# Mirrored score blocks of a fused attention and MLP block, turned by VectorE and DMA instead of TensorE

## The chip, the core and the metric

The kernel runs on one core of a Trainium2 chip. The core has TensorE (matrix products), VectorE, ScalarE and GpSimd (elementwise work), each with an instruction queue of its own that it works through in order, and SyncE (SP), whose queue here issues every DMA. The metric is the time of one execution in device microseconds (us). Three runs give 693.47, 693.54 and 694.78 us, median 693.54.

## What is computed

Eight batches of 1024 rows and 256 features pass through attention and an MLP, each behind a layer norm with a modulation per batch. All is float32.

```
mod = (_silu(L0_c) @ L0_wmod).reshape(L0_c.shape[0], 6, 1, -1)
sa, ca, ga, sb, cb, gb = (mod[:, 0], ..., mod[:, 5])
h = _layernorm(x) * (1 + ca) + sa
lhs, rhs = h * w_lhs, h * w_rhs
scores = einsum('nsd,ntd->nst', lhs, rhs)
attn = softmax(scores, axis=2)
x = x + ga * einsum('nst,ntd->nsd', attn, h)
h = _layernorm(x) * (1 + cb) + sb
x = x + gb * (relu(h @ W1 + b1) @ W2 + b2)
```

Since lhs and rhs are the same h times a factor per feature, the score matrix is symmetric: block (i, j) of 128 by 128 is block (j, i) turned.

## The kernel before

**Tiling.** A batch is 8 row tiles of 128 rows, so the scores of a batch are 8 × 8 blocks in the tile `S`. The features are two halves of 128 (`DK`), the hidden layer 8 tiles of 128, taken over two halves of 512 rows: 16 steps each of the first layer (F) and the second (G). For accuracy every product is made of three matmuls: hi × hi, hi × lo, lo × hi, where hi is a value rounded to fp32r and lo the rest.

**Stages.** Each engine has a list of steps, a kind and a number: `BEFORE_STEPS`, `FIRST_STEPS` (batch 0), `SECOND_STEPS` (batch 1), `STEPS` (batches 2 to 6, a loop), `LAST_STEPS` (batch 7), `AFTER_STEPS`. A suffix "-" means that the step works for the batch before, "+" for the one after: the MLP of a batch runs beside the attention of the next. Every engine goes through its list in order; between engines stand only semaphore waits. Batch 0 goes a way of its own in plain float32.

**The kinds, batches 1 to 7.**
- SC.n, TensorE (L542 to L585): scores of row tile n into one of two PSUM tiles `score`. Rows 0 to 3 make the left half from column `first_col[n]` on (0, 1, 2, 2 blocks in) and all of the right half; rows 4 to 7 only the right half, from 4, 5, 6, 6. What stands left of that start is the mirror of blocks already made and is turned by TensorE with the identity (L584). SC.n waits until VectorE has copied SC.n−2 out (`scores_read`).
- SC.n, VectorE (L864): copies the scores to `S` and takes each row's maximum over them into `row_max`.
- ST.n, VectorE (L896): turns 32 × 32 pieces of the right half of rows 0 to 3 into `stage`. SW and SR, SP (L444, L449): write the stage to DRAM and read it back piece by piece into `lower`, the lower left quarter of the matrix.
- MX, VectorE (L900, L903): the maximum over `lower`, joined to `row_max` of rows 4 to 7.
- MB.0 and MB.1, TensorE (L655): spread the maxima of rows 0 to 3 and 4 to 7 over all partitions, into `max_ps`.
- SB.n, VectorE (L887 to L892): subtracts the maxima from columns n of `S`, in place. EX.n, ScalarE (L793): exponential, in place. SM.n: ScalarE rounds it to `Phi` (L806), VectorE makes the rest `Plo` (L911). AV.n: TensorE multiplies with `V` (L690 to L694), VectorE divides and adds to x (L928) and takes the statistics of the second norm.
- VN, ScalarE (L783): x minus mean into `ln_v`; VL, VectorE (L1038): times rstd and gate, four instructions of one tile each; V: the hi part by ScalarE (L788), the lo part by VectorE (L980).
- L1 and L2: mean and variance on VectorE (L951, L954), −mean and rstd on GpSimd (L1069 to L1072). N1 and N2, GpSimd (L1079): normalise four tiles of 256 columns into `ln_t`. BH and B2, VectorE (L990, L991): turn 32 × 32 pieces of it. SH, RH, S2, R2, SP: carry them through DRAM (`blocks`, `block_rows`). TH and T2: ScalarE and VectorE make the turned features of the attention (`Lhi`, `Rhi`, `Llo`, `Rlo`) and the MLP (`h2hi`, `h2lo`).
- F.n: product on TensorE (L593 to L595), ReLU and hi part on ScalarE (L715, L719), lo part on GpSimd (L1088). G.n: product on TensorE (L530 to L536). OUT, VectorE (L1026, L1030): gate and sum. XG, VectorE (L1051): x plus the gated bias. XC, GpSimd (L1139): x plus the shift of the attention. X0, X1, XT, AM, GA, GB, O0, O1 on SP: loads and stores. WS: ScalarE and GpSimd split the weights, in batch 0; WR: TensorE waits for that. TP: TensorE turns the features of the first MLP half of batch 0.

Of the kernel before, what the change touches and what calls it, by code (L numbers as in the profile page):

```python
# [5 lines left out]
F32 = mybir.dt.float32  # L6
F32R = mybir.dt.float32r
ALU = mybir.AluOpType
# [90 lines left out]
        SC.0 F.0- SC.1 F.1- F.2- SC.2 SC.3 F.3- SC.4 F.4- MB.0 G.0- SC.5 G.1- SC.6 F.5- SC.7 G.2- F.6- G.3-  # L99
        G.4- F.7- G.5- F.8- F.9- G.6- F.10- MB.1 G.7- AV.0 F.11- AV.1 G.8- F.12- G.9- AV.2 G.10- AV.3 F.13-  # L100
        F.14- AV.4 F.15- G.11- AV.5 G.12- AV.6 G.13- G.14- G.15- AV.7
    """,
    "act": """
        F.0- VN.0 F.1- V.0 F.2- T2.1- F.3- VN.1 F.4- EX.0 L1.0+ SM.0 F.5- EX.1 F.6- F.7- EX.2 F.8- V.1 F.9-
        EX.3 SM.1 F.10- TH.0+ SM.2 SM.3 F.11- EX.4 EX.5 SM.4 F.12- SM.5 F.13- TH.1+ F.14- EX.6 MC.0 SM.6
        EX.7 SM.7 F.15- T2.0
    """,
    "dve": """
# [1062 lines left out]
```

## Time and profile before

| | |
|---|---|
| median of three runs | 693.54 us (693.47 to 694.78) |
| profiled execution, its span | 691.5 us (its own time is not given apart) |
| TensorE busy | 686.1 us, 99% |
| VectorE busy | 558.4 us, 81% |
| ScalarE busy | 427.5 us, 62% |
| GpSimd busy | 361.7 us, 52% |
| one middle batch | 82.2 us |
| granted TensorE clock | full in all slices |

The profile is one execution, and its span runs from the first to the last instruction. PE is TensorE's matmuls, DVE VectorE, ACT ScalarE, POOL GpSimd, SP SyncE. Busy time is a union: consecutive instructions overlap a little in the records, since the end of one lies behind the start of the next. So what an instruction in a row costs its engine is the distance to the next start. Idle time of an engine that others don't wait for costs nothing.

### The profile page before, as it was taken

Reading aid. Unit: us, or ns where it says so; the run is one execution under the profiler, and the core shown is the slowest. Engines: PE = TensorE matmul, PEld = TensorE weight load, DVE = VectorE, ACT = ScalarE, POOL = GpSimd, SP = SyncE. Lnnn points to the kernel's source line nnn. Section 1 sums busy time; section 2 is a strip of 40 time slices with the busy share of each in tenths; the row PEclk is TensorE's granted clock in tenths of the full one; section 3 lists DMA queues with packets and bytes.
Section 4 is the critical chain, followed back from the end, with each engine's and each line's share of the span. In section 5 each row is a group of like instructions: output and inputs, shape, how many; then the busy total and the mean of one; then the engine's idle time right before and its main releaser. Section 6 shows DMA issues by size and latency. Waiting matters only on the chain.

```text
span 691.5 us, 13488 instructions
## 1 busy us (share of the span) xinstructions
PE 686.1 (99%) x4621; PEld 627.7 (91%) x4621; DVE 558.4 (81%) x1059; ACT 427.5 (62%) x625; POOL 361.7 (52%) x396
## 2 busy tenths in 40 slices
PE   9999999999999999999999999999999999999998
PEld 8688899998999989998999989999899998999997
DVE  5699989799898898978989799887989887876421
ACT  3265398736786367683786647864678634845562
POOL 3572576636654386352872458643665434523644
PEclk9999999999999999999999999999999999999999
DMA  8211761137431382315622266112843126003300
GB/s 294 81 49 59 204 193 55 39 107 252 123 100 56 103 232 91 99 61 179 180 67 90 67 226 185 61 38 98 258 121 99 46 91 221 1 1 100 100 31 30
DMA packets 61663, 77.54 MB, mean 112 GB/s; under 512 B 5632, under 2 KB 54336, under 8 KB 61632
## 3 DMA queue, kind: packets, MB, share of 16 engines
q1 hardware_dynamic: 61632, 77.14, 35.5%
q8 instruction: 18, 0.29, 0.2%
q14 instruction: 13, 0.11, 0.1%
HBM read 46.15 MB, written 30.97 MB: 112 GB/s over the span
## 4 chain that ended last, share of the span: by engine, by line
PE 94%; DVE 4%; issue 0%; ACT 0%; DMA 0%; DVEq 0%; ACTq 0%; SPq 0%
PE col L595 9%; PE col L594 9%; PE col L593 9%; PE acc L530 8%; PE acc L531 8%; PE acc L536 8%; PE score L694 8%; PE score L690 8%; PE score L691 8%; PE score L578 4%; PE score L579 4%; PE score L580 4%; PE score L576 2%; PE score L584 2%; PE score L499 1%; DVE S L879 1%
## 5 line engine op out<-in xcount | busy, mean ns | idle before, releaser
L1088 POOL TENSOR_TENSOR hid_lo<-hid,hid_hi 128x512 fp32r<-128x512 f32 x127 | 175.4, 1386 | 143.2 <-ACT hid_hi L719 142.8
L715 ACT ACTIVATE hid<-col,b1T 128x512 f32<-128x512 f32 x128 | 87.0, 679 | 140.3 <-PE col L595 126.1
L530 PE MATMUL acc<-W2hi,hid_hi 128*128 128x256 f32 x480 | 119.2, 282 | 0.0
L531 PE MATMUL acc<-W2lo,hid_hi 128*128 128x256 f32 x480 | 116.9, 278 | 0.0
L690 PE MATMUL score<-V,Phi 128*128 128x258 f32 x448 | 108.8, 281 | 0.0
L691 PE MATMUL score<-V,Phi 128*128 128x256 f32 x448 | 108.6, 281 | 0.0
L719 ACT ACTIVATE hid_hi<-hid 128x512 fp32r<-128x512 f32 x128 | 81.0, 633 | 37.6 <-PE acc L536 29.8
L593 PE MATMUL col<-h2hi,W1hi 128*128 128x512 f32 x256 | 102.4, 400 | 0.0
L595 PE MATMUL col<-h2hi,W1lo 128*128 128x512 f32 x256 | 101.0, 395 | 0.0
L594 PE MATMUL col<-h2lo,W1hi 128*128 128x512 f32 x256 | 100.6, 393 | 0.0
L530 PEld LDWEIGHTS acc<-W2hi,hid_hi 128*128 128x128 f32 x480 | 90.4, 188 | 2.1
L531 PEld LDWEIGHTS acc<-W2lo,hid_hi 128*128 128x128 f32 x480 | 90.2, 188 | 1.8
L690 PEld LDWEIGHTS score<-V,Phi 128*128 128x128 f32 x448 | 85.0, 190 | 0.7
L691 PEld LDWEIGHTS score<-V,Phi 128*128 128x128 f32 x448 | 84.0, 188 | 0.6
L1069 POOL TENSOR_SCALAR nm<-mv 128x4 f32<-128x4 f32 x32 | 16.7, 523 | 129.2 <-DVE mv L932 104.2
L911 DVE TENSOR_TENSOR Plo<-S,Phi 128x1024 fp32r<-128x1024 f32 x56 | 70.2, 1269 | 8.1 <-ACT Phi L806 6.4
L536 PE MATMUL acc<-W2hi,hid_lo 128*128 128x256 f32 x480 | 76.6, 276 | 0.0
L864 DVE TENSOR_SCALAR_CACHE_REDUCE S<-score 128x1024 f32<-128x1024 f32 (+1 forms) x64 | 62.7, 980 | 15.2 <-PE score L584 12.9
L793 ACT ACTIVATE S<-S 128x1024 f32<-128x1024 f32 (+1 forms) x64 | 64.4, 1019 | 13.2 <-DVE S L879 7.7
L1139 POOL TENSOR_TENSOR x_cur<-x_cur,attn_mod 128x512 f32<-128x512 f32 x32 | 43.3, 1354 | 40.8 <-DVE ln_v L1038 40.8
L536 PEld LDWEIGHTS acc<-W2hi,hid_lo 128*128 128x128 f32 x480 | 64.6, 188 | 0.0
L694 PE MATMUL score<-V,Plo 128*128 128x258 f32 x448 | 62.8, 282 | 0.0
(139 smaller groups left out, 1493.2 us busy)
## 6 DMA issues: line engine op xcount, KB each, us to landing
block_rows<-blocks SPq DMA_DIRECT2D x29, 512.0 KB, 2.9
blocks<-block_rows SPq DMA_DIRECT2D x116, 128.0 KB, 3.0
x_cur<-x SPq DMA_DIRECT2D x16, 512.0 KB, 3.9
ln_t<-x SPq DMA_DIRECT2D x14, 512.0 KB, 4.8
score_blocks<-stage SPq DMA_DIRECT2D x14, 512.0 KB, 4.2
lower<-score_blocks SPq DMA_DIRECT2D x56, 128.0 KB, 2.9
out<-x_mlp SPq DMA_DIRECT2D x8, 512.0 KB, 3.0
out<-x_mlp SPq DMA_DIRECT2D x15, 256.0 KB, 2.2
```

The source lines that it names most:

```text
L530: nc.tensor.matmul(o, hi, W2hi[:, it, :], start=(it == 0 and (apart or t % 2 == 0)), stop=False, skip_group_check=True)
L531: nc.tensor.matmul(o, hi, W2lo[:, it, :], start=False, stop=False, skip_group_check=True)
L536: last = nc.tensor.matmul(o, lo, W2hi[:, it, :], start=False, stop=(it == FT - 1), skip_group_check=True)
L593: nc.tensor.matmul(col[n % 2][:], W1hi[:, kk, tile], h2hi[:, kk, cols], start=(kk == 0), stop=False)
L594: nc.tensor.matmul(col[n % 2][:], W1hi[:, kk, tile], h2lo[:, kk, cols], start=False, stop=False)
L595: last = nc.tensor.matmul(col[n % 2][:], W1lo[:, kk, tile], h2hi[:, kk, cols], start=False, stop=(kk == DK - 1))
L690: nc.tensor.matmul(o, Phi[:, slot, t, :], V[:, t, 0:VW], start=(t == 0), stop=False)
L691: nc.tensor.matmul(o[:, 0:D], Phi[:, slot, t, :], V[:, t, VP:VP + D], start=False, stop=False)
L694: last = nc.tensor.matmul(o, Plo[:, slot, t, :], V[:, t, VP:VP + VW], start=False, stop=(t == T - 1))
L715: nc.scalar.activation(hid[:, n % 2, :], col[n % 2][:], ACT.Relu, bias=b1T[:, n % FT:n % FT + 1]).then_inc(col_read, 1)
L719: nc.scalar.activation(hid_hi[:, n % RING, :], hid[:, n % 2, :], ACT.Copy).then_inc(hid_hi_done, 1)
L1088: G.tensor_tensor(hid_lo[:, n % RING, :], hid[:, n % 2, :], hid_hi[:, n % RING, :].bitcast(F32), ALU.subtract).then_inc(hid_lo_done, 1)
```

## The change

In batches 1 to 7 TensorE turns no score blocks. It multiplies the right upper quarter whole, and of the two quarters on the diagonal the blocks `QCOLS`: (0, 1, 2), (1, 2, 3), (2, 3), (0, 3) of each row, 10 where it were 11. Six blocks of each quarter are mirrors: VectorE turns their 32 × 32 pieces (QT.0, QT.1, out of `S` into `stage_q`), SP writes them to DRAM (QW) and reads them back piece by piece (QR) into `turned_in`. `S` is packed, so that these blocks fit into it. The maxima have parts (`part_max`): from the copies, from the turned blocks (MX.0 and MX.2) and from the lower left quarter (MX.1); MB.0 and MB.1 both wait for them (`max_ready`). SB reads from `S` and the turned blocks and writes to a ring `soft` of three column tiles, on which EX and SM work. N1 and N2 go from GpSimd to ScalarE, with scale rstd and bias `nb1`, `nb2` = −mean × rstd, a product that GpSimd adds. VN does the whole normalisation, and VL is one instruction for four tiles. All orders are new; batch 0 keeps its steps otherwise.

```diff
 STEPS = {
     "pe": """
-        SC.0 F.0- SC.1 F.1- F.2- SC.2 SC.3 F.3- SC.4 F.4- MB.0 G.0- SC.5 G.1- SC.6 F.5- SC.7 G.2- F.6- G.3-
...
+        SC.0 SC.1 F.0- F.1- SC.2 SC.3 F.2- F.3- SC.4 SC.5 G.0- G.1- F.4- SC.6 G.2- G.3- SC.7 F.5- F.6- MB.0
...
     "sp": """
-        AM.0 GA.0- S2.1- XT.0+ SW.0 R2.1- SR.0 X1.0 SW.1 SR.1 SH.0+ XT.1+ RH.0+ O0.0- SH.1+ RH.1+ GB.0 S2.0
...
+        AM.0 S2.1- XT.0+ R2.1- QW.0 X1.0 SW.0 QR.0 SR.0 SH.0+ SW.1 XT.1+ SR.1 GA.0- RH.0+ QW.1 GB.0 QR.1 SH.1+
...
+    QCOLS = [(0, 1, 2), (1, 2, 3), (2, 3), (0, 3)]
...
+                    elif kind == "QW":
+
+                        sp.wait_ge(quarter_done[n], b)
+                        sp.dma_start(quarter_blocks[n], stage_q[n]).then_inc(quarter_stored[n], 16)
+                    elif kind == "QR":
+
+                        sp.wait_ge(quarter_stored[n], 16 * b)
+                        for u in range(Q):
...
+                        for right in range(0 if n < HT else 1, 2):
...
+                            if not right:
+                                o = score[n % 2][:, 0:HR]
+                            else:
+                                o = score[n % 2][:, HR:HR + len(quarter) * P]
...
+                                elif n % HT == HT - 1:
+                                    whole = slice(n // HT * HR, (n // HT + 1) * HR)
+                                    hi, lo = [r[:, kk, whole].rearrange("p (c q) -> p c q", q=P)[:, ::HT - 1, :] for r in (Rhi, Rlo)]
...
-                        for i in range(left // P, at // P):
-                            if i == at // P - 1:
-                                pe.wait_ge(scores_read, T * b + i + 1)
-                            last = nc.tensor.transpose(score[n % 2][:, i * P:(i + 1) * P], S[:, i, n * P:(n + 1) * P], ident[:])
...
+                            pe.wait_ge(max_ready, 2 * b + n - 1)
...
+                    elif kind == "N1":
+                        act.wait_ge(ln1_rstd, 2 * b + 3 + n)
+                        for t in range(HT):
+                            i = n * HT + t
+                            last = nc.scalar.activation(ln_t[:, t, :], ln_t[:, t, :], ACT.Identity, scale=rs1[:, i:i + 1], bias=nb1[:, i:i + 1])
+                        last.then_inc(ln1_done, 1)
...
+                        V_.tensor_tensor(tile[:, h * HT:(h + 1) * HT][:, rows], kept, most.broadcast_to(list(kept.shape)), ALU.subtract)
...
+                        V_.tensor_tensor(by_quarter(out), turned_q[h][:, turns], by_quarter(most.broadcast_to(list(out.shape))), ALU.subtract)
...
+                    elif kind == "QT":
+
+                        dve.wait_ge(scores_read, T * b + (n + 1) * HT)
...
-                        for t in range(HT):
-                            i = n * HT + t
-                            dve.wait_ge(v_mean, HT * (2 * b + n - 2) + t + 1)
-                            V_.scalar_tensor_tensor(ln_v[:, t, :], ln_v[:, t, :], rs1[:, i:i + 1], attn_mod[:, 0, :], ALU.mult, ALU.mult).then_inc(v_ln, 1)
+                        dve.wait_ge(v_mean, HT * (2 * b + n - 2) + HT)
+                        V_.tensor_tensor(ln_v[:], ln_v[:], attn_mod[:, 0:1, :].broadcast_to([P, HT, D]), ALU.mult).then_inc(v_ln, HT)
```

How the instructions now stand, at three places of the loop body. First TensorE at the end of SC.3; score0 and score1 are the two PSUM tiles, col1 that of the first layer. Before, the end of the products, two transposes, then step F.3:

```order
L580 MATMUL score1<-Rhi,Llo 128x512
L584 MATMUL score1<-ident,S 128x128 x2
L590 REGISTER_ALU
L593 MATMUL col1<-h2hi,W1hi 128x512
L594 MATMUL col1<-h2lo,W1hi 128x512
```

After, the right half of SC.3 is the product of blocks 0 and 3, and step F.2 follows:

```order
L634 MATMUL score1<-Rhi,Lhi 128x256
L635 MATMUL score1<-Rlo,Lhi 128x256
L636 MATMUL score1<-Rhi,Llo 128x256
L642 REGISTER_ALU
L645 MATMUL col0<-h2hi,W1hi 128x512
L646 MATMUL col0<-h2lo,W1hi 128x512
```

The transposes are gone, and the step ends with a product.

Second, TensorE around MB.0, whose instruction writes the maxima to score1. Before, F.4 stands ahead of it and G.0 behind it:

```order
L595 MATMUL col0<-h2hi,W1lo 128x512
L648 REGISTER_ALU
L655 MATMUL score1<-ident,row_max 128x128 x4
L520 ISA
L530 MATMUL acc<-W2hi,hid_hi 128x256
```

After, F.6 stands ahead and G.4 behind:

```order
L647 MATMUL col0<-h2hi,W1lo 128x512
L703 ISA
L712 MATMUL score1<-ident,row_max 128x128 x4
L568 MATMUL acc<-W2hi,hid_hi 128x256
L569 MATMUL acc<-W2lo,hid_hi 128x256
```

MB.0 moved from between SC.4 and SC.5 to behind SC.7, and its wait is now one for `max_ready`.

Third, VectorE from the copy of SC.7 on. Before, SB.0 and SB.1 stand ahead of it, and BH.0, SB.2, VL.1 behind it:

```order
L864 TENSOR_SCALAR S,row_max<-score 128x512
L364 REGISTER_ALU
L990 STREAM_TRANSPOSE blocks<-ln_t 128x4x4x32
L991 STREAM_TRANSPOSE blocks<-ln_t 128x4x4x32
L889 TENSOR_TENSOR S<-S,score 128x4x128
L890 REGISTER_ALU
L892 TENSOR_TENSOR S<-lower,score 128x4x128
L1037 ISA
L1038 SCALAR_TENSOR_TENSOR ln_v<-ln_v,rs,attn_mod 128x256
```

After, BH.0 (L1119, L1120) stands ahead of the copy, and behind it MX.0, VL.1, QT.1, SB.0 and V.1:

```order
L1120 STREAM_TRANSPOSE blocks<-ln_t 128x4x4x32
L947 REGISTER_ALU
L956 TENSOR_SCALAR S,part_max<-score 128x256
L1029 REGISTER_ALU
L1031 TENSOR_REDUCE part_max<-S 128x3x2
L1036 TENSOR_REDUCE row_max<-part_max 128x4
L1164 ISA
L1165 TENSOR_TENSOR ln_v<-ln_v,attn_mod 128x1024
L1017 STREAM_TRANSPOSE stage_lr<-S 128x6x4x32
L995 TENSOR_TENSOR soft<-S,score 128x2x128
L999 TENSOR_TENSOR soft<-S,score 128x256
L1003 TENSOR_TENSOR soft<-S,score 128x512
```

The first subtraction moved behind all copies and the maxima, and it is three instructions.

## Rows read from the trace of the kernel before

**Rows 1.** The page: span, busy time by engine, chain that ended last

```profile
span 691.5 us, 13488 instructions
...
PE 686.1 (99%) x4621; PEld 627.7 (91%) x4621; DVE 558.4 (81%) x1059; ACT 427.5 (62%) x625; POOL 361.7 (52%) x396
...
PE 94%; DVE 4%; issue 0%; ACT 0%; DMA 0%; DVEq 0%; ACTq 0%; SPq 0%
```

**Rows 2.** Stretch, length; busy PE, PEld, DVE, ACT, POOL; clock, DMA share, GB/s

```profile
69.00:640.00 571.00, 570.88 (x3951) 529.65 (x3950) 491.17 (x902) 373.48 (x545) 302.65 (x321) 1.00 0.37 116
233.60:315.80 82.20, 82.20 (x572) 76.32 (x571) 71.56 (x133) 54.67 (x80) 44.36 (x48) 1.00 0.40 121
```

**Rows 3.** All waits of TensorE: total us, times, longest

```profile
PE score L499 <- POOL ident L1062: 1.5, 1, 1.5
PE score L683 <- DVE x_cur L926: 0.3, 1, 0.3
```

**Rows 4.** Timeline of TensorE, middle batch: start us, length us, instruction

```profile
237.67 0.33 PE L579 MATMUL score<-Rlo,Lhi 128*128 128x384 f32 x1
237.84 0.33 PE L580 MATMUL score<-Rhi,Llo 128*128 128x384 f32 x1
238.02 0.39 PE L578 MATMUL score<-Rhi,Lhi 128*128 128x512 f32 x1
238.25 0.40 PE L579 MATMUL score<-Rlo,Lhi 128*128 128x512 f32 x1
...
239.40 0.27 PE L584 MATMUL score<-ident,S 128*128 128x128 f32 x1
...
251.05 0.60 PE L655 MATMUL score<-ident,row_max 128*128 128x128 f32 x4
```

**Rows 5.** Timeline of VectorE, middle batch; in brackets idle time ahead and its end

```profile
243.00 1.63 DVE L1038 SCALAR_TENSOR_TENSOR ln_v<-ln_v,rs,attn_mod 128x256 f32<-128x256 f32 x4
244.55 0.68 DVE L1051 TENSOR_TENSOR x_mlp<-x_cur,gb_b 128x512 f32<-128x512 f32 x1
...
255.44 0.68 DVE L892 TENSOR_TENSOR S<-lower,score 128x512 f32<-128x512 f32 x1
256.04 0.68 DVE L889 TENSOR_TENSOR S<-S,score 128x512 f32<-128x512 f32 x1
...
264.88 2.27 DVE L900 TENSOR_REDUCE left_max<-lower 128x4 f32<-128x2048 f32 x1
...
281.82 1.18 DVE L887 TENSOR_TENSOR S<-S,score 128x1024 f32<-128x1024 f32 x1
282.93 0.15 DVE L917 RECIPROCAL inv_sum<-score 128x1 f32<-128x1 f32 x1
...
315.29 0.17 DVE L917 RECIPROCAL inv_sum<-score 128x1 f32<-128x1 f32 x1 [1.58 <-PE score L694]
```

**Rows 6.** Timeline of ScalarE, middle batch: VN

```profile
254.43 1.69 ACT L783 ACTIVATE ln_v<-x_cur,nm 128x256 f32<-128x256 f32 x4
```

**Rows 7.** GpSimd: N1 over three batches (busy us, mean ns); timeline of statistics

```profile
L1079 POOL TENSOR_SCALAR ln_t<-ln_t,nm,rs 128x256 f32<-128x256 f32 x24 | 13.0, 560 | 0.7 <-POOL rs L1072 0.7
...
251.38 1.16 POOL L1069 TENSOR_SCALAR nm<-mv 128x4 f32<-128x4 f32 x1
...
253.22 1.02 POOL L1072 TENSOR_TENSOR rs<-var_eps,half_power 128x4 f32<-128x4 f32 x1
```

**Rows 8.** Timeline of SP's DMA issues, middle batch; the page's time to landing

```profile
243.10 0.33 SPq L444 DMA_DIRECT2D score_blocks<-stage  x1
...
246.91 1.73 SPq L449 DMA_DIRECT2D lower<-score_blocks  x4
...
lower<-score_blocks SPq DMA_DIRECT2D x56, 128.0 KB, 2.9
```

**Rows 9.** Two VectorE lines, batches 1 to 7: shortest, median, longest in ns

```profile
L997 DVE SCALAR_TENSOR_TENSOR Llo<-featT,wl,Lhi x20: 736/746/1786, 206.1 to 553.2; 128x512 fp32r<-128x512 f32 x20
L980 DVE TENSOR_TENSOR V<-ln_v,V x12: 1217/1474/1660, 168.4 to 598.9; 128x1024 fp32r<-128x1024 f32 x12
```

More of the change, by code:

```diff
@@ L559, in part @@
                             pe.wait_ge(scores_read, T * b + n - 1)
[L560 to L570 removed]
+                        tile = slice(n * P, (n + 1) * P)
@@ new lines, in part @@
+                        if ph is PH["first"]:
+                            at = first_col[n]
+                            for lo_col in range(0, ROWS, HR):
+                                start_col = max(at, lo_col)
+                                width = lo_col + HR - start_col
+                                if width <= 0 or n == 0 and lo_col == 0:
+                                    continue
+                                o, cols = score[n % 2][:, start_col:lo_col + HR], slice(start_col, lo_col + HR)
+                                for kk in range(DK):
+                                    last = nc.tensor.matmul(o, L_first[:, kk, tile], R_first[:, kk, cols], start=(kk == 0), stop=(kk == DK - 1))
+                            for i in range(at // P):
+                                if i == at // P - 1:
+                                    pe.wait_ge(scores_read, T * b + i + 1)
+                                last = nc.tensor.transpose(score[n % 2][:, i * P:(i + 1) * P], S[:, i, n * P:(n + 1) * P], ident[:])
+                            last.then_inc(scores_done, 1)
+                            continue
@@ L789, in part @@
                     elif kind == "EX":
-                        tile = S[:, HT if ph is PH["first"] and n < HT else 0:T, n * P:(n + 1) * P]
+                        if ph is PH["first"]:
+                            tile = S[:, HT if n < HT else 0:T, n * P:(n + 1) * P]
+                        else:
+                            tile = soft[:, n % RING, :, :]
                         act.wait_ge(sub_done, T * b + n + 1)
@@ L1064, in _, with statistics @@
             pool.wait_ge(const_ready, 1)
-            def statistics(mv, nm, rs, h, eps_done, rstd_done, count):
+            def statistics(mv, nm, rs, nb, h, eps_done, power_done, rstd_done, count):
                 tiles = slice(h * HT, (h + 1) * HT)
```

310 lines of the change are left out of this document (183 added, 127 removed).

## The prediction

> **What bounds the kernel now.** I read the page first: TensorE is busy 99% of the 691.5 us, VectorE 81%, ScalarE 62%, GpSimd 52%, and the chain that ended last is 94% TensorE [rows 1]. Busy TensorE alone is not yet a bound, so the stages come next [rows 2]: from 69 to 640 us it is busy for 570.88 of 571.00 us, and 82.20 of 82.20 us in a middle batch, at the full granted clock (1.00, 2.4 GHz). What TensorE waited for is two waits, 1.8 us together [rows 3], so neither lies in that stretch. TensorE issues one stream, in a written order, without a pause. What leaves the stream is a gain one to one; anything else can only lose, by making it wait. VectorE works 71.56 us of the same 82.20, ScalarE 54.67, GpSimd 44.36 [rows 2].
>
> The span lies 2.0 us under the median of the three runs (693.5); the profiled execution has no time of its own beside it. I sum against the span and carry the 2.0 us.
>
> **What TensorE loses.** *Turned blocks.* In each of the seven batches 1 to 7 (batch 0 keeps its old path) the old step SC turned 1, 2, 2 blocks for rows 1, 2, 3 and 1, 2, 2 again for 5, 6, 7: 10 transposes. Their price is the distance between starts, not their duration, since records overlap: four in a row take 0.60 us, one alone lasts 0.27, so (0.60 − 0.27) / 3 = 0.11 us [rows 4]. 10 × 0.11 = 1.10 us. *Narrower products.* Rows 0 and 4 multiply 384 columns instead of 512 (the two blocks of "36 for 38"): 2 rows × 2 halves of the features × 3 matmuls = 12. Starts of 512 columns lie 0.23 us apart, of 384 columns 0.35 / 2 = 0.175 [rows 4]. 12 × 0.055 = 0.66 us. Rows 3 and 7 still multiply 256 columns. Together 1.76 us a batch, 7 × 1.76 = **12.3 us**; F, G, AV and MB keep their counts.
>
> A rule speaks for less. The trace has 0.11 us for a transpose of 128 columns [rows 4]. The Trainium skill (TensorE: Matmul & The Clock Gate, "Wait — 56ns, not 53.3ns?") gives a warm gap of columns / 2.4 GHz + 2.5 ns, which is 56 ns for 128 columns and 53 ns between 512 and 384. By it the estimate would be 7 × (0.56 + 0.64) = 8.4 us. The 53 agrees with the rows, the 56 does not, and the row decides.
>
> *One thing no row shows:* rows 3 and 7 read the moving operand as two separate pieces of 128 columns (blocks 0 and 3). Either that is free, or at the far end each of these 12 matmuls of 256 columns takes twice its 0.12 us (half of 0.23): 1.4 us a batch, 9.9 in all. A gain is excluded, the columns being as many. I take nothing: the nearest rows, at two widths, follow the column count alone.
>
> **What the others gain.** For work in a row on VectorE I use distances between starts: 512 columns 0.60 us, 1024 columns 1.11 [rows 5], so 1.0 us for 1000 columns and 0.09 an instruction.
> - Copy out of PSUM (SC): 4608 columns for 6144, one more instruction: −1.5 + 0.1 = −1.4.
> - The new transposes QT: 2 × 768 columns: +1.7. The stage transposes stay.
> - Maxima (MX): the reduction of 2048 takes 2.27 us [rows 5], 1.1 for 1000; 1536 more columns 1.7, four more small instructions 0.5: +2.2.
> - Subtraction (SB): the same columns in 24 instructions for 12: +1.1.
> - VL: two instructions of 1024 columns for eight of 256. Four take 1.55 us [rows 5], so 3.1 becomes 2.2: −0.9.
>
> Sum +2.7: VectorE goes to **74.3 us of a period of 80.4**. Bounds: +1.0 if the reductions go at the copies' 1.0 and their small instructions vanish in overlap, +5 if each of the 19 added instructions costs 0.2 us.
>
> ScalarE takes 16 normalising steps of 256 columns, four in 1.69 us [rows 6]: at most +6.8, so 61.4. GpSimd sheds 8.7 us (13.0 over three batches, and as much again for N2 [rows 7]) and adds four tiny products: 36.5. SP gets ten more issues a batch of 0.43 us (four in 1.73 [rows 8]).
>
> All this lies beside TensorE and costs nothing while no TensorE instruction waits. But VectorE's idle time falls from 10.6 to 6.1 us, the cover gets thin, and so I walked a middle batch (us from the start of SC.0):
> 1. *SC.6 waits for the copy of SC.4* (two score banks). TensorE, from the end of SC.3 at 11.8: F.2 F.3 SC.4 SC.5 G.0 G.1 F.4 = 3 × 1.38 + 2 × 1.04 + 2 × 1.37 = 9.0 (six matmuls of 0.23, six of 0.175, twelve of 0.114). VectorE: copy 1.0, QT 0.9, four ST 2.5, XG 0.6, V 1.5, L1 1.7, copy 0.45: 8.65. Slack 0.3.
> 2. *MB.0 now waits for the quarter blocks.* QT.0 ends at 13.8. On SP the write QW.0 stands ahead of X1 and SW.0, the read QR.0 behind them. A round trip of the stage takes 8.4 us today: issued at 243.10, last read issued at 248.64, 2.9 to land [rows 8]. So the blocks are there by 22.2; MB.0 stands at 27.7, behind F.6. Slack on that way 4. But MX.0 is queued behind BH.0 on VectorE, and BH.0 needs ScalarE's N1.0, which needs GpSimd: L1.0 ends at 20.0, the statistics take up to 2.9 (251.38 to 254.24 [rows 7]), N1.0 1.7, BH.0 1.2, copy SC.7 0.35, MX.0 1.1: 27.3. Slack 0.4.
> 3. *Batch end.* T2.0 on VectorE ends about 4.0 into the next batch, F.0 stands at 4.8. N2.1, first on ScalarE, ends at 4.6 at the latest, before F.0's product (6.2). SC.2 (7.6) needs the copy of SC.0, done at 6.3.
> 4. *Batch 0:* TensorE has the same work. WS moves behind XC.3 on GpSimd and ends near 56, WR stands at 67. TP moves behind AV.7; T2.0 is through at 71.5, F.0 of batch 1 stands at 72.4. No wait.
> 5. *Tail:* behind the last AV.7, N2.1 ends at 5.8, B2.1 at 7.0, the DMA at 15.4 (8.4 again), T2.1 at 18.8; F.8 stands at 19.2.
>
> Crossings with 0.3 to 0.8 us of slack: I grant 0.15 us a batch, 1.0 in all. **Forecast: 693.5 − 12.3 + 1.0 = 682.2**; inside this case 680.5 to 684.
>
> **Rivals.**
> *A, part of the gain turns into TensorE waits at SC.6 and MB.0.* For it: the slacks, and single VectorE instructions that reach 1.79 us for a median of 0.75 (L997), or 1.66 for a least of 1.22 (L980) [rows 9]; one such hit costs 0.4 to 1.0 us. Against it: GpSimd has a fifth less to collide with. At 0.4 to 1.2 us a batch, 7 × 0.8 = 5.6: 687. Both stretched forms read two SBUF tensors. The Trainium skill (SBUF — State Buffer, "Who interferes with whom") tells of an exclusive lock between GpSimd and such VectorE instructions, and of a port of its own for ScalarE. The stretched rows agree with it.
>
> *B, VectorE becomes the bound: slower.* Much of its idle time is round trips through ScalarE (V, Plo), which it cannot shorten. If it keeps all 10.6 us beside 74.3 of work, the period is 84.9, 2.7 above today's: 693.5 + 7 × 2.7 = 712. It decides from 82.2 − 74.3 = 7.9 us of own idle time on. Against it: 1.58 us at once are a wait for AV's product [rows 5], and such waits vanish when VectorE is late.
>
> *C, the split operand costs double:* 682.2 + 9.9 = 692.1.
>
> *D, the transposes hide half their price.* If what stands behind them takes up half of each 0.11 us, 70 × 0.055 = 3.9 us less is gained: 686. The page's 8.4 us above would end there too.
>
> **How the numbers follow.** Chances: forecast 0.65, A 0.20, B 0.06, C 0.04, D 0.05. The range takes in the forecast's own, D and all but the top of A, and at the low end the 1.0 us granted and the 1.8 us of old waits: 679.5 to 688.5; B, C and the top of A (0.05) stay out. Within 0.2% of 693.5 (1.4 us, about what a measurement can tell from no change) lies half of C, 0.02; slower are B and a hair of C, 0.07; faster is the rest, 0.91.
>
> **What the profile after would show.** No transposes in SC, 384 columns in rows 0 and 4, a middle batch of 80.4 us with TensorE equal to its length: forecast. TensorE waiting for a copy of scores or for row_max: A, and where. VectorE above 92% of the batch and TensorE waiting in many places: B. Starts in rows 3 and 7 more than 0.12 us apart: C. I am wrong if over 0.3 us a batch is lost at a place not listed, or if the granted clock falls.

## The result: 698.9 us against 694.0, and the profile after

The changed kernel takes 698.93 us (median of four runs), the kernel before took 693.98 beside it: a ratio of 1.0076, 95% interval 1.0063 to 1.0089. It is 5 us slower where 11 us less were forecast.

The page of the changed kernel: span, busy time by engine, and the chain that ended last.

```profile
span 697.3 us, 13519 instructions
...
PE 684.3 (98%) x4551; PEld 622.0 (89%) x4551; DVE 560.5 (80%) x1158; ACT 496.9 (71%) x745; POOL 295.0 (42%) x308
...
PE 51%; DVE 23%; issue 10%; ACT 7%; POOL 7%; DVEq 0%; ACTq 0%; DMA 0%; POOLq 0%; SPq 0%
```

Against [rows 1], TensorE issues 70 instructions fewer (10 × 7, as the change says), VectorE is as busy as before, ScalarE has 69 us more, GpSimd 67 less. What changed in kind is the last line: the chain was 94% TensorE, now a half of it runs through the others.

A middle batch from one SC.0 to the next, columns as in [rows 2]:

```profile
317.25:401.19 83.94, 82.45 (x561) 75.40 (x561) 72.51 (x147) 64.22 (x98) 35.77 (x36) 1.00 0.44 137
```

It is 83.9 us long. The same stretch before was 82.24; the forecast was 80.4. Over the five middle batches that is 7.7 us more (418.9 us for 411.2; the first of them is 0.6 us shorter than the rest); the rest of the program is 1.9 us shorter in the spans. TensorE stands idle for 1.5 us by this row, and in the list of its waits:

```profile
PE score L634 <- DVE S L956: 3.4, 5, 0.7
PE acc L574 <- POOL hid_lo L1209: 1.6, 5, 0.3
PE score L537 <- POOL ident L1189: 1.5, 1, 1.5
PE score L747 <- DVE x_cur L1057: 1.1, 5, 0.2
```

That is 6 us over five batches, and it explains only part of the 17 us lost there (418.9 us for 5 × 80.4). The rest hides in the records: the modelled end of a matmul lies some 0.16 us (512 columns) behind the start of the next, so a shorter wait leaves no idle time, and a longer one shows that much too short. I therefore took start-to-start distances, minus those of an undisturbed pair, for every matmul of this batch:

| TensorE starts late at | released by | late, us |
|---|---|---|
| SC.6 | VectorE's copy of SC.4 | 0.85 + 0.11 |
| AV.6 | VectorE's AV.4, behind B2.0 | 0.38 + 0.10 |
| G.3, its hid_lo | GpSimd, F.3 behind the statistics of L1.0 | 0.48 + 0.11 |
| SC.0 | TH.1 of this batch | 0.30 + 0.10 |
| F.0 | T2.0 | 0.28 + 0.10 |
| AV.7 | Plo | 0.16 + 0.11 |
| MB.1 | row_max | 0.18 |
| G.0 | XG.3 | 0.07 + 0.11 |

The second number is the matmul behind the first late one, whose start is 0.10 to 0.11 us late too, in all rows but that of MB.1. Together 3.4 us, which is what the batch lost. MB.0, at 347.18, starts on time.

The stretch before the largest of them, on VectorE, then GpSimd, then ScalarE (start, length, instruction, idle time ahead):

```profile
332.12 0.67 DVE L1009 STREAM_TRANSPOSE stage<-S 128x512 f32<-128x512 f32 x1
332.72 1.71 DVE L1178 TENSOR_TENSOR x_mlp<-x_cur,gb_b 128x512 f32<-128x512 f32 x1
...
336.17 1.18 DVE L1109 TENSOR_TENSOR V<-ln_v,V 128x1024 fp32r<-128x1024 f32 x1
337.27 1.39 DVE L1080 BATCH_NORM_STATS2 stats<-ln_t 128x6 f32<-128x256 f32 x4
338.58 0.40 DVE L1083 BATCH_NORM_AGGREGATE mv<-stats 128x2 f32<-128x6 f32 x4
338.93 0.56 DVE L956 TENSOR_SCALAR_CACHE_REDUCE S<-score 128x384 f32<-128x384 f32 x1
...
344.09 0.71 DVE L1119 STREAM_TRANSPOSE blocks<-ln_t 128x512 f32<-128x512 f32 x1 [2.57 <-ACT ln_t L874]
```

```profile
332.59 1.29 POOL L1209 TENSOR_TENSOR hid_lo<-hid,hid_hi 128x512 fp32r<-128x512 f32 x1 [4.29 <-ACT hid_hi L776]
...
341.64 0.20 POOL L1201 TENSOR_TENSOR nb<-nm,rs 128x4 f32<-128x4 f32 x1
341.80 1.28 POOL L1209 TENSOR_TENSOR hid_lo<-hid,hid_hi 128x512 fp32r<-128x512 f32 x1
```

```profile
339.21 2.08 ACT L840 ACTIVATE ln_v<-x_cur,nb,rs 128x256 f32<-128x256 f32 x4 [1.67 <-DMA x_cur<-x]
341.88 2.08 ACT L874 ACTIVATE ln_t<-ln_t,nb,rs 128x256 f32<-128x256 f32 x4 [0.58 <-POOL nb L1201]
343.86 0.67 ACT L772 ACTIVATE hid<-col,b1T 128x512 f32<-128x512 f32 x1
```

Four things are to be seen. XG.3 (L1178) takes 1.71 us beside GpSimd's hid_lo, where 0.65 to 0.69 is usual. V.0 (L1109) and L1.0 (L1080, L1083) stand ahead of the copy of SC.4 (L956). On ScalarE VN.1 (L840), N1.0 (L874) and the hidden layer F.4 (L772) stand in a row, and four normalising steps take 2.08 us, not the 1.69 of [rows 6]. And VectorE stands idle 2.57 us for N1.0 before BH.0.

### The profile page after: what moved, and what is told of

Same layout as the page of the kernel before. It is cut to its first block, busy times and chain, and to the rows that moved or that the text cites. A ratio compares the mean times of both kernels' runs of the same rounds, so it can differ in the third digit from the quotient of the medians.

```text
span 697.3 us, 13519 instructions
## 1 busy us (share of the span) xinstructions
PE 684.3 (98%) x4551; PEld 622.0 (89%) x4551; DVE 560.5 (80%) x1158; ACT 496.9 (71%) x745; POOL 295.0 (42%) x308
## 4 chain that ended last, share of the span: by engine, by line
PE 51%; DVE 23%; issue 10%; ACT 7%; POOL 7%; DVEq 0%; ACTq 0%; DMA 0%; POOLq 0%; SPq 0%
PE col L645 6%; PE col L647 6%; PE col L646 5%; PE acc L574 4%; PE acc L568 4%; PE acc L569 4%; PE score L740 4%; DVE x_cur L1057 3%; POOL rs L1199 2%; PE score L634 2%; DVE stats L1059 2%; PE score L747 2%; PE score L751 2%; PE score L748 2%; PE score L635 2%
## 5 line engine op out<-in xcount | busy, mean ns | idle before, releaser
L772 ACT ACTIVATE hid<-col,b1T 128x512 f32<-128x512 f32 x128 | 86.6, 677 | 43.8 <-PE col L647 41.4
L853 ACT ACTIVATE soft<-soft 128x1024 f32<-128x1024 f32 x56 | 59.1, 1056 | 30.7 <-DVE soft L1006 23.3
L1040 DVE TENSOR_TENSOR Plo<-soft,Phi 128x1024 fp32r<-128x1024 f32 x56 | 67.5, 1220 | 14.3 <-ACT Phi L869 14.3
L1196 POOL TENSOR_SCALAR nm<-mv 128x4 f32<-128x4 f32 x32 | 8.2, 256 | 166.9 <-DVE mv L1061 113.5
L634 PE MATMUL score<-Rhi,Lhi 128*128 128x512 f32 (+2 forms) x168 | 57.6, 343 | 4.0 <-DVE S L956 3.4
L869 ACT ACTIVATE Phi<-soft 128x1024 fp32r<-128x1024 f32 x56 | 58.4, 1051 | 0.8
```

Source lines behind the costliest of these rows:

```text
L772: nc.scalar.activation(hid[:, n % 2, :], col[n % 2][:], ACT.Relu, bias=b1T[:, n % FT:n % FT + 1]).then_inc(col_read, 1)
```

## The experiments

Theories. **S**: ScalarE's normalising (longer than reckoned, and in the chain to the block turns) holds VectorE, and through it TensorE. **V**: VectorE's own added work is the bound. **G**, later **P**: single collisions and the places of single steps in the new orders make the waits. Times are medians; "before" stood at 693.4 to 694.3 beside all of them. The half-width of the intervals is 0.10 to 0.17% of a time, so a difference of 1 us between two kernels is hardly one.

### Is the saving on TensorE real?

e4: the kernel before, its orders untouched, with TensorE's new work alone.

```diff
-                            o = score[n % 2][:, start_col:lo_col + HR]
+                            end = lo_col + HR - (P if ph is not PH["first"] and (n, lo_col) in ((0, 0), (4, HR)) else 0)
+                            o = score[n % 2][:, start_col:end]
...
-                        for i in range(left // P, at // P):
+                        for i in range(left // P, at // P if ph is PH["first"] else 0):
```

> The kernel before with only TensorE's work of the change: in batches 1 to 7 no block is turned (its columns of the score tile keep what stood there, so the mirrored blocks are left out of what is computed), and rows 0 and 4 multiply 384 columns. Orders, VectorE, ScalarE and GpSimd as before. The sum of the prediction expects 7 times 1.76 = 12.3 us less: 681.5 us, or up to 684 with new small waits. If the transposes hide half of their price: 686 us. If the old kernel was bound by its ring of other engines as well, at 82.2 us a batch by chance: 690 us or more.

682.85 us, ratio 0.9850 (0.9833 to 0.9866). Its middle batch:

```profile
310.00:390.56 80.56, 80.56 (x562) 75.16 (x561) 73.10 (x132) 54.67 (x80) 44.62 (x48) 1.00 0.40 123
```

TensorE gives 82.24 − 80.56 = 1.7 us a batch, 10.6 in all, and stays busy for the whole batch although VectorE has 73.1 us of work, more than in the changed kernel. So the 1.76 us a batch of the forecast were right, and the loss comes from the rest of the change: 698.93 − 682.85 = 16 us, with the same work on TensorE.

### ScalarE, VectorE or GpSimd?

e1: rstd is left out of all of ScalarE's normalising steps (one of three such lines is shown).

```diff
-nc.scalar.activation(ln_t[:, t, :], ln_t[:, t, :], ACT.Identity, scale=rs1[:, i:i + 1], bias=nb1[:, i:i + 1])
+nc.scalar.activation(ln_t[:, t, :], ln_t[:, t, :], ACT.Identity, bias=nb1[:, i:i + 1])
```

> The changed kernel with the scale operand left out of ScalarE's N1, N2 and VN (24 steps a batch keep only their bias), so the rstd is left out of what is computed; everything else stands. Four steps take 2.08 us with the scale and took 1.69 us without it. Theory S (ScalarE's normalising, slower and in the chain to BH and B2, holds VectorE and through it TensorE): six groups of four lose 0.4 us each, of which three or four lie on the ring; the middle batch falls from 83.9 to 82.3 to 83.0 us, the time from 698.9 to 688 to 693 us. Rival V (VectorE's own added work sets the pace): under 0.5 us a batch, 696 us or more. Rival G (one or two single places, XG beside GpSimd and XC behind the statistics): about 0.5 us a batch, 695 us.

686.15 us (0.9895, 0.9879 to 0.9912). The line of N1 in the changed kernel, then in this one (busy us, mean ns):

```profile
L874 ACT ACTIVATE ln_t<-ln_t,nb,rs 128x256 f32<-128x256 f32 x56 | 29.0, 589 | 15.7 <-POOL nb L1201 15.7
```

```profile
L874 ACT ACTIVATE ln_t<-ln_t,nb 128x256 f32<-128x256 f32 x56 | 23.8, 496 | 16.8 <-POOL nb L1201 16.8
```

The scale costs 0.093 us a step. There are 176 such steps, 16.4 us of ScalarE's time in all, and the kernel became 12.8 us shorter, more than the 6 to 11 that theory S had expected. But one thing more had changed in the trace: XG.3 no longer met GpSimd's hid_lo (L1178 at a mean of 683 ns for 849). So this run favours S without clearing G.

e6 leaves the scale out of N1 and N2 alone (the same edit in two of the three lines); e5 keeps ScalarE's N1 and N2 and gives V's scaling back to VectorE.

```diff
-nc.scalar.activation(ln_v[:, t, :], x_cur[:, i, :], ACT.Identity, scale=rs1[:, i:i + 1], bias=nb1[:, i:i + 1]).then_inc(v_mean, 1)
+nc.scalar.activation(ln_v[:, t, :], x_cur[:, i, :], ACT.Identity, bias=nm1[:, i:i + 1]).then_inc(v_mean, 1)
-V_.tensor_tensor(ln_v[:], ln_v[:], attn_mod[:, 0:1, :].broadcast_to([P, HT, D]), ALU.mult).then_inc(v_ln, HT)
+V_.scalar_tensor_tensor(ln_v[:, t, :], ln_v[:, t, :], rs1[:, i:i + 1], attn_mod[:, 0, :], ALU.mult, ALU.mult).then_inc(v_ln, 1)
```

> Leaves rstd out of the normalising of h1 and h2 alone (N1, N2: Identity with bias only), V keeps its scale. ScalarE is freed of 16 x 0.094 / 2 = 0.75 us a batch at exactly the steps that VectorE's block turns wait for. Theory S: most of the 12.5 us that the run without any scale gained comes back, 686 to 689. If it is ScalarE's load in general and not these steps, half of it, 692. Theory V: no gain, 698.

> Only the normalising for V goes back to the old form: ScalarE adds the negated mean alone (no scale), and VectorE applies rstd and the modulation in four operations. ScalarE is freed of 4 x 2 x 0.094 = 0.75 us a batch, VectorE gets about 4 x 2 x 0.4 - 2 x 1.23 = +0.7 us a batch. Theory S (what holds VectorE and TensorE is ScalarE's normalising ahead of the block turns of h1 and h2, which stays): 697 to 699, no change worth telling. Theory V (VectorE's own work): about 0.7 x 7 = 5 us slower, 703. If the V branch were the seat of what the first run without scale gained: 690 or below.

e6: 693.39 us, 5.5 less than the changed kernel. XG.3 still takes its 1.7 (mean of L1178 847), so these 5.5 belong to the operand that ScalarE's 120 steps lost. It is the outcome written down for ScalarE's load in general (692), not that of S (686 to 689). e5: 705.03, 6.1 us more. S had said no change and is wrong there; V's 703 is nearer. In its trace VL.0 takes 1.67 us for 1.23 and VL.1 2.71, and TensorE newly waits 0.8 and 0.4 us for hidden layers that ScalarE's V.1, held by VL.1, has kept back.

e8 takes work from VectorE at one place, the maxima.

```diff
-... turned_q[h].rearrange("p (g j) u r -> p g j u r", j=2), AX.XY, ALU.max)
+... turned_q[h].rearrange("p (g j) u r -> p g j u r", j=2)[:, :, :, 0:1], AX.XY, ALU.max)
-by_row = lower.rearrange(
+by_row = lower[:, 0:1].rearrange(
```

> Leaves out part of the reductions of the maxima: MX.0 and MX.2 read one quarter of their turned blocks and MX.1 one half of its own, so the maxima are those of a part of the scores; all writes, waits and queues stay. VectorE is freed of about 2 x 0.65 + 1.2 = 2.5 us a batch, 17 us in all, between the scores and the first exponentials. Theory V (VectorE is the bound, its idle is fixed): 682. Theory S: VectorE waits for ScalarE's normalising, and work taken from it away from those waits turns into idle time: 695 to 699.

697.14 us: 14 us less busy VectorE (546.3 for 560.5), 1.8 less time. Its middle batch, with 70.56 of VectorE for 72.51, is 83.6 long, and the late starts at SC.6, G.3, AV.6 and SC.0 are as large as before. V is refuted as the bound: 14.2 us of VectorE's work gone gave 1.8 us. In e5 12.0 us more of busy VectorE went with 6.1 us of time, so it depends on where the work stands; how much of the 6.1 is VectorE's alone was not separated, since ScalarE's VN changed with it.

e2 gives N1 and N2 back to GpSimd right behind its statistics, e9 half of them (two tiles of four); both are in the new orders. The middle batches' GpSimd row of e2 (ScalarE's steps N1 and N2 are gone there):

```diff
-        F.0- F.1- F.2- L1.0+ F.3- F.4- F.5- F.6- F.7- XC.0 F.8- L1.1+ F.9- F.10- F.11- F.12- XC.1 L2.0 XC.2
+        N2.1- F.0- F.1- F.2- L1.0+ N1.0+ F.3- F.4- F.5- F.6- F.7- XC.0 F.8- L1.1+ N1.1+ F.9- F.10- F.11- F.12- XC.1 L2.0 N2.0 XC.2
```

> The changed kernel with N1 and N2 back on GpSimd, right behind L1 and L2, as instructions of the old form; VN keeps its scale. Theory S: ScalarE loses 8.3 us of work a batch and nothing queues N behind F; VectorE's waits for ln_t fall from 5.1 us a batch to 1 to 2, the batch to 82 to 83 us, the time to 686 to 693 us, though GpSimd's lo parts come later by up to 2.2 us each. Rival V: no gain, 698 us or more, since GpSimd also collides with VectorE again. Rival G: about 699 us or slower, since XC and hid_lo are now behind N on GpSimd.

> N1 and N2 are shared: ScalarE normalises the first two tiles of each half, GpSimd the other two right behind its statistics (the block turn waits for both). ScalarE is freed of 4 x 2 x 0.588 = 4.7 us a batch, GpSimd gets 8 operations, which took 1.5 us each and more where it did all of them (before, and in the run with all on GpSimd). Theory S (ScalarE's share is too late): the chain to each block turn is 2 x 0.59 on ScalarE and some 3 us on GpSimd beside it, so GpSimd is now the later one by about 0.7 us: 695 to 705; if ScalarE's wait for its turn in its queue was what cost, 690 or below. Since all of it on GpSimd cost 33 us more, a result above 705 would say that any normalising on GpSimd in these orders is late.

731.64 us for e2, far above what any theory had reckoned with (the highest said about 699 or slower), and 698.24 for e9, as good as the changed kernel. With all of it on GpSimd, TensorE waited 14.9 us for Plo and 13.3 for hid_lo. With half of it, 8.1 us for hid_lo:

```profile
PE acc L571 <- POOL hid_lo L1214: 8.1, 6, 1.6
PE score L631 <- DVE S L953: 2.7, 4, 0.7
```

ScalarE had 4 us less in the batch, and GpSimd's hidden low parts came too late instead: one wait for another. In these orders, freeing ScalarE helped only where the work went nowhere else. (The expectation of e9 priced one such GpSimd operation at 1.5 us; their means are 577 and 606 ns in the kernel before and 554 and 774 in e9, so that its time fell into the range of S says little for the sum.)

e3 moves XC.2 and XC.3 on GpSimd ahead of L2.0 (the row of the middle batches is shown).

```diff
-        F.0- F.1- F.2- L1.0+ F.3- F.4- F.5- F.6- F.7- XC.0 F.8- L1.1+ F.9- F.10- F.11- F.12- XC.1 L2.0 XC.2
-        F.13- XC.3 F.14- F.15- L2.1
+        F.0- F.1- F.2- L1.0+ F.3- F.4- F.5- F.6- F.7- XC.0 F.8- L1.1+ F.9- F.10- F.11- F.12- XC.1 XC.2 XC.3 L2.0 F.13- F.14- F.15- L2.1
```

> The changed kernel with XC.2 and XC.3 ahead of L2.0 in GpSimd's order in batches 1 to 7, nothing else. Now XC.3 ends at 390.04 and AV.4 and AV.6 on VectorE start right behind it. Rival G expects 0.4 to 1.0 us a batch, 692 to 696 us. Theory S: B2.0 stands ahead of AV.4 on VectorE and waits for N2.0 anyway, so under 0.3 us a batch, or slightly slower since L2.0 comes later: 697 to 700 us. Rival V: no difference.

707.88 us, 9 more, outside all that was expected. XC's additions now met VectorE's TH (mean of its two lines 929 and 900 ns for 746 and 744), 9.5 us in all, and TensorE waited 5.6 us for Phi and 4.1 for x_cur. XC's old place was not what cost. The new one shows that two collisions a batch can cost nearly what the whole change is worth; the part of L2.0, which now comes later, was not separated.

### Which places?

All of these edit the orders of the middle batches alone. e11, e12 and e13, each row cut to the steps around the move:

```diff
 e11, VectorE
-        SM.3 AV.1 SB.4 TH.0+ SB.5 AV.2 AV.3 XG.0 SM.4 SM.5 SB.6 B2.0 AV.4 SM.6
+        SM.3 AV.1 SB.4 TH.0+ SB.5 AV.2 AV.3 XG.0 SM.4 SM.5 SB.6 AV.4 B2.0 SM.6
 e12, VectorE
-        QT.0 ST.0 XG.3- ST.1 ST.2 ST.3 V.0 L1.0+ SC.4
+        QT.0 ST.0 ST.1 ST.2 ST.3 XG.3- V.0 L1.0+ SC.4
 e13, VectorE, ScalarE, GpSimd
-        ST.3 V.0 L1.0+ SC.4 T2.1-
+        ST.3 L1.0+ SC.4 V.0 T2.1-
-        L1.0+ VN.1 N1.0+ F.4-
+        L1.0+ N1.0+ VN.1 F.4-
-        F.2- L1.0+ F.3-
+        F.2- F.3- L1.0+
```

> The order of the middle batches alone: VectorE takes AV.4 before the block turn B2.0 instead of behind it. In the changed kernel VectorE stands idle 1.1 us before B2.0 (it waits for ScalarE's N2.0), AV.4's operations (1.3 us) are queued behind, and TensorE then waits 0.5 us for them before AV.6; VectorE reaches the end of the batch that much late, where TensorE waits 0.4 us at SC.0 and 0.4 us at F.0. Theory P (small waits that the places of single steps make; each can be moved away): 5 batches x up to 1.3 us, 692 to 696. Theory S (only less ScalarE work helps): VectorE waits all the same, 698 to 699.

> The order of the middle batches alone: XG.3 moves behind ST.3 on VectorE, away from GpSimd's hid_lo of F.2, beside which it took 1.71 us instead of 0.65. Theory G (this one collision starts the wait for the copy of SC.4 before SC.6, 0.96 us a batch): 5 x 0.96 = 4.8, 694. Theory S: 698 to 699, since VectorE has 2.6 us idle right behind those copies.

> The orders of the middle batches alone, around L1.0: VectorE takes L1.0 and SC.4 before V.0, ScalarE N1.0 before VN.1, GpSimd F.3 before the statistics of L1.0, where it stands idle 5 us. TensorE's waits at SC.6 (0.96 us a batch) and for hid_lo of F.3 (0.5) should go, and N1.0 end 1 us earlier. Theory P: 5 x 1.45 = 7, 691 to 694. Theory S: 698. What could turn it: VN.1 and VL.1 come 2 us later, ahead of the first exponentials.

e14 is all three together.

> The orders of the middle batches with all of it: AV.4 before B2.0, XG.3 behind ST.3, L1.0 and SC.4 before V.0, N1.0 before VN.1, F.3 before L1.0 on GpSimd. Theory P: the waits add, 5 x (0.96 + 0.5 + 0.5 + 0.8) = 13.8 at most, 685 to 690, which would be faster than the kernel before. If the time moves by less than half of that, the waits only change place and the engines between them (VectorE and ScalarE in turn) set the pace: 692 to 698.

e11: 694.62 us, 4.3 less: one step moved over one other gives back nearly half of what the change had lost. The late starts at SC.0 vanish with it. B2.0 in the changed kernel, then in e11, where ScalarE is done when VectorE reaches it:

```profile
388.62 0.71 DVE L1119 STREAM_TRANSPOSE blocks<-ln_t 128x512 f32<-128x512 f32 x1 [1.10 <-ACT ln_t L888]
```

```profile
387.17 0.71 DVE L1119 STREAM_TRANSPOSE blocks<-ln_t 128x512 f32<-128x512 f32 x1
```

e12: 697.90, 1.0 less. XG.3 is short again, but TensorE stops at a wait that no one had in mind, since G.0 needs XG.3:

```profile
PE acc L568 <- DVE x_mlp L1178: 3.1, 5, 0.6
```

e13: 704.79, 5.9 more where 5 to 8 less were expected, e14: 700.34, above both of its ranges. TensorE in e13:

```profile
346.95 0.40 PE L647 MATMUL col<-h2hi,W1lo 128*128 128x512 f32 x1
349.85 0.79 PE L645 MATMUL col<-h2hi,W1hi 128*128 128x512 f32 x1 [2.50 <-ACT hid L772]
350.44 0.63 PE L646 MATMUL col<-h2lo,W1hi 128*128 128x512 f32 x1
350.86 0.63 PE L647 MATMUL col<-h2hi,W1lo 128*128 128x512 f32 x1
351.29 0.63 PE L645 MATMUL col<-h2hi,W1hi 128*128 128x512 f32 x1
```

and the stretch from the end of that wait (columns as above, the third from the end is the granted clock):

```profile
349.80:352.60 2.80, 2.75 (x7) 2.07 (x8) 2.37 (x4) 2.75 (x4) 2.07 (x2) 0.50 1.02 341
```

The half clock is no part of the 5.9 us. It followed this wait and that at 178.07, while behind the equal waits at 264.74, 436.26 and 521.32 the clock stayed full. And the profiled execution, of 706.81 us at a mean granted clock of 0.995, is the slowest of four; the others, at 1.000, took 704.70 to 704.83.

ScalarE in e13, ahead of that wait:

```profile
345.18 2.08 ACT L874 ACTIVATE ln_t<-ln_t,nb,rs 128x256 f32<-128x256 f32 x4 [4.75 <-POOL nb L1201]
347.16 2.06 ACT L840 ACTIVATE ln_v<-x_cur,nb,rs 128x256 f32<-128x256 f32 x4
349.13 0.67 ACT L772 ACTIVATE hid<-col,b1T 128x512 f32<-128x512 f32 x1
```

N1.0 (L874) stood in front and waited for GpSimd's statistics, VN.1 (L840) no longer filled that time, and F.4 (L772) came behind both: TensorE waited 2.5 us for the hidden layer. From this I took theory **C**: the pace is set by a chain V.0 (VectorE), VN.1, N1.0, F.4 (ScalarE), with BH.0 and MB.0 behind it.

Four kernels take e13 apart. e16 is e11 with GpSimd's F.3 ahead of L1.0; e17 adds VectorE's part of e13 (V.0 behind SC.4, ScalarE as it was); e15 adds XG.3 ahead of QT.0; e18 is e15 without the scale.

> AV.4 before B2.0 as in the run that gained by it, and on GpSimd F.3 ahead of L1.0, in the middle batches. TensorE's wait for hid_lo of F.3 (0.49 us a batch) should go. Theory P: 5 x 0.49 = 2.4 off 694.6: 692. If another wait stands right behind it: 694.6 again.

> As the run before it, and on VectorE L1.0 and SC.4 before V.0 (1.2 us), with ScalarE's order as it was (VN.1 before N1.0). TensorE's wait for the copy of SC.4 before SC.6 (0.95 us a batch) should go: Theory P: 5 x 0.95 off 692: 687.5. What cost e13 its 5.9 us was then the move on ScalarE alone (TensorE waited 2.5 us a batch for the hidden layer behind N1.0); if L1.0 or V.0 were the cause, this run is above 695.

> As the run before it, and XG.3 ahead of QT.0, where GpSimd is idle (the other place tried, behind ST.3, made TensorE wait for XG.3 before G.0). VectorE gets 1.06 us a batch back before SC.4. If the wait at SC.6 is gone already, this changes little: 686 to 688; if V.0's move did not suffice, up to 5 us faster than the run before it.

> As the run before it (e15), with rstd left out of all ScalarE normalising as in the first run (bias only, 494 ns for 588). If both causes are separate and add: about 12 us below e15, but TensorE's own work sets a floor near the 682 that the old kernel with the new TensorE work took: 680 to 683. If mended orders had already made room for the slower form: within 2 us of e15.

e16: 694.47, nothing. The late start at G.3 is gone, and 0.27 us turned up at MB.0 and 0.18 at a hidden layer. e17: 700.49, 6.0 more, e15: 699.68, e18: 692.46. The expectation of e17 had put e13's cost down to ScalarE's order alone and was wrong; its other branch, above 695 if L1.0 or V.0 were the cause, came true, and the rows below point to V.0. e15 gains 0.8 us where 686 to 688 were expected, or up to 5 us: moving XG.3 ahead of QT.0 is worth little while V.0 stands behind SC.4. e18 is 7.2 us below e15, between the 12 and the 2 that were written down. ScalarE in e17, then in e16:

```profile
337.28 0.19 ACT L810 ACTIVATE mod_a<-mod_cols 128x4 f32 x1
339.92 2.08 ACT L840 ACTIVATE ln_v<-x_cur,nb,rs 128x256 f32<-128x256 f32 x4 [2.45 <-DVE V L1109]
342.20 2.08 ACT L874 ACTIVATE ln_t<-ln_t,nb,rs 128x256 f32<-128x256 f32 x4 [0.20 <-POOL nb L1201]
```

```profile
334.67 0.19 ACT L810 ACTIVATE mod_a<-mod_cols 128x4 f32 x1
336.26 2.08 ACT L840 ACTIVATE ln_v<-x_cur,nb,rs 128x256 f32<-128x256 f32 x4 [1.40 <-DMA x_cur<-x]
```

In e17 VN.1 waits 2.45 us for V.0, where in e16 it waited 1.40 us for the transfer of x, and all behind it shifts; TensorE's wait at SC.6 is gone, and waits at MB.0 (3.0 us in all) and for hidden layers (5.4) have come. V.0 and SC.4 both want to be first on VectorE, so the way out is to take time from what stands before both.

e19 does that: the changed kernel with AV.4 before B2.0 and XG.3 before QT.0, where GpSimd is idle. e20 is e19 without the scale.

```diff
-        SC.3 QT.0 ST.0 XG.3- ST.1 ST.2 ST.3 V.0 L1.0+ SC.4
+        SC.3 XG.3- QT.0 ST.0 ST.1 ST.2 ST.3 V.0 L1.0+ SC.4
```

> The changed kernel with two steps of VectorE moved in the middle batches: AV.4 before B2.0, and XG.3 ahead of QT.0 (0.65 us there instead of 1.71 beside GpSimd); V.0, L1.0 and SC.4 keep their order, ScalarE and GpSimd too. Everything from ST.1 to BH.0 comes up to 1.06 us earlier, V.0 with it, so both TensorE's wait at SC.6 (0.95 us a batch) and the chain V.0, VN.1, N1.0, F.4 shrink. Theory C (this chain through ScalarE is the pace): 5 x 0.95 off 694.6, 690, faster than the kernel before. If ScalarE's VN.1 is held by the transfer of x instead (it waited 1.4 us for it), BH.0 gains less and TensorE waits at MB.0: 692 to 695.

> As the run before it, with rstd left out of all ScalarE normalising (bias only, 494 ns for 588). Changed kernel without scale took 686.2. If the two causes add, 12 us below the run before it, but not below TensorE's floor of some 680 to 682: 680 to 683. If orders and form free the same wait: 686.

e19 took **688.98 us**, a ratio of 0.9926 (0.9913 to 0.9940): faster than both kernels, with the whole computation kept. e20 took 683.17 (0.9848, 0.9832 to 0.9864). A middle batch of e19, then of e20:

```profile
313.35:395.28 81.93, 81.45 (x563) 75.39 (x561) 71.50 (x147) 64.20 (x97) 35.24 (x36) 1.00 0.46 141
```

```profile
309.43:390.59 81.16, 81.05 (x561) 75.35 (x561) 71.28 (x147) 62.06 (x98) 35.06 (x36) 1.00 0.47 142
```

In e19 the late start at SC.6 is gone. VectorE's busy time fell by the 1.0 us of the collision, and it does the same work. XG.3 in its new place has its short length:

```profile
327.13 0.69 DVE L1178 TENSOR_TENSOR x_mlp<-x_cur,gb_b 128x512 f32<-128x512 f32 x1
```

One way from the changed kernel to what its TensorE's work is worth (e4) thus has three steps: AV.4's place 4.3 us (e11), XG.3's place 5.6 (e19 against e11), the scale 5.8 (e20 against e19). That leaves 0.3 of the 16 us, so orders and scale together are the whole loss. The first two are faults of the new orders, the third is the price of the moved normalising.

But these shares hold for this way alone, since the causes do not add. The two moves by themselves give 9.9 us (e19), the scale by itself 12.8 (e1); together they give 15.8 and not 22.7. So some 7 us of waits go with either of them. A part of that is seen: in e1 XG.3 stopped meeting hid_lo although no step was moved. e20's expectation had 12 us for causes that add and 686 us for causes that free the same wait; 683.17 lies between.

## Why the forecast was wrong, point by point

- **What TensorE loses: right.** 12.3 us were reckoned, e4 gave 10.6; 1.7 us a batch for 1.76. Most of the missing part lies outside the middle batches.
- **VectorE's sum: right in what mattered.** 74.3 us a batch were forecast, 72.5 came, near the low bound of +1.0. With GpSimd lighter, the two stretched lines of [rows 9] shrank in the middle batches (V from a mean of 1483 ns to 1192, Llo from 1003 to 746), which the sum had not taken in.
- **ScalarE's term: mis-sized.** "Four in 1.69 us, at most +6.8" took its price from VN [rows 6], which has a bias and no scale. With the scale four take 2.08, and ScalarE gained 64.2 − 54.7 = 9.5. The step was called an upper bound and was none. The Trainium skill (ScalarE: Activation LUTs, "What ACT_TABLE_LOAD costs") states 93 ns for each operand of one value per partition; the 93 ns between the two rows of L874 agree, and looking it up would have given the term. In time it was worth 12.8 us in the changed orders (e1) and 5.8 in the mended ones (e20). The prediction let it cost nothing, as all that lies beside TensorE.
- **The failed step: "I grant 0.15 us a batch, 1.0 in all"** for the crossings. It was 3.5 us a batch and 16 in all (e4 against the changed kernel). The 0.15 was a guess that no row gave. The walk found the two places, SC.6 and MB.0, with slacks of 0.3 and 0.4, and took each duration at its usual value. MB.0 came on time. At SC.6 a collision (XG.3, 1.71 for 0.65) and 0.37 us of idle time before VL.0 met a slack of 0.3: 0.96 us late, in each batch. A fixed order repeats its collision in every batch; it is no chance event that hits now and then. The trace before had shown that already: the longest of L997 in [rows 9] is no stray value. Five of the line's 20 take 1.78 to 1.79 us, one in each middle batch, 82.24 us apart, each begun while GpSimd was in a hid_lo. Two of them:

```profile
206.10 1.78 DVE L997 SCALAR_TENSOR_TENSOR Llo<-featT,wl,Lhi 128x512 fp32r<-128x512 f32 x1
...
288.34 1.78 DVE L997 SCALAR_TENSOR_TENSOR Llo<-featT,wl,Lhi 128x512 fp32r<-128x512 f32 x1
```
- **Places not listed.** AV.6 (AV.4 queued behind B2.0, which waits for N2.0), hid_lo behind the statistics, SC.0 behind TH.1. The prediction had said it was wrong if over 0.3 us a batch was lost at such a place; it was 2.1 by the table (G.3, AV.6, SC.0, AV.7, MB.1, G.0). I had walked what waits for the moved steps, and not what stands in the queue behind each step that now waits for ScalarE.
- **Rival A (0.20, 687)** had the mechanism and the first place, at a quarter of the loss. **Rival B (0.06, 712)** had the sign: VectorE did keep its idle time, 83.9 − 72.5 = 11.4 us a batch for 10.6 before, since the waits for ScalarE (2.57 us before BH.0) took the place of those that shrank. But VectorE was not the bound, as e8 shows, so the sign was right for another reason. **C** did not happen: the 256-column matmuls of rows 3 and 7 start 0.12 us apart. **D** is at most the 1.7 us between 12.3 and 10.6.
- **Batch end, batch 0, tail:** everything outside the five middle batches was 1.9 us shorter than before, with 3.5 us less TensorE work in it: close to what the walk said, not all of it. The end of the batch was not: SC.0 and F.0 start 0.8 us late.

What stays open: e20's middle batches are 0.6 us longer than e4's (81.16 for 80.56), 2.6 us over the five, while its time is only 0.3 longer, so outside them it is some 2 us shorter; no run tells why. Nor was it tried whether batch 7 and the tail would gain by such moves, or what N1 and N2 on GpSimd would cost in orders made for it.

## What to carry to other kernels

When TensorE issues without a pause, each instruction taken from it counts nearly in full (10.6 of 12.3 us here), but a change that also rewrites the orders stakes more than it wins: one step in the wrong place cost 4 to 6 us here, the whole saving was 11. Walk, for every step that gets a new or slower producer, what is queued behind it on its engine and who waits for that; and price an instruction by a row with the same operands, not the same name. Two moves helped here: a step let past a neighbour that has to wait anyway (e11), and time taken from what stands ahead of a wait (e19). Exchanging two steps that are both waited for only shifted the wait and cost 6 us (e17), and freeing the engine elsewhere gave little (e8). What two mends give together has to be measured, since each can free the same wait.

## What the runs showed of the hardware

- ScalarE's ACTIVATE of 256 columns with a bias from memory takes 496 ns, with a scale from memory too 589.
- XG.3, a VectorE operation with two inputs in SBUF, began at 332.72, 0.13 us into GpSimd's hid_lo (332.59 to 333.88), and ended 0.55 us after it: 1.71 us for 0.65 to 0.69. The transpose that ran into the same hid_lo, with one input, kept its 0.67. The Trainium skill (SBUF — State Buffer, "Who interferes with whom") tells of an exclusive lock for such pairs, and these rows agree. With VectorE first it was GpSimd that took longer: V.1 began at 350.07 and kept its 1.21 us, the hid_lo that began at 350.44 took 2.00 for 1.29.
- After a wait of 2.5 us TensorE can go on at half its clock, but need not. In e13 it did so behind the one that ended at 349.85: a granted 0.50 (1.2 GHz) for 2.8 us, starts 0.42 to 0.43 us apart for 0.23, which by these starts is an estimated 1.3 us beyond the wait's length. It did so behind one more of the five equal waits, and behind the other three the starts stood 0.23 apart at once. So they did behind the five late starts of 1.9 us in e14.
- The second matmul after a wait starts 0.10 to 0.11 us late as well, in seven of the eight late starts of the table above.
